# Two of a decoder layer's layer norms applied by ScalarE instead of VectorE

## The reference

```python
x = x + _L0_attn_ref(_layernorm(x), ...)      # selective scan: 512 channels, 16 states
x = x + _L0_xattn_ref(_layernorm(x), ctx_1024, ...)
x = x + _L0_ffn_ref(_layernorm(x), ...)       # RMS norm, top 2 of 8 experts

# the first part, per batch row:
xp, z = jnp.split(x @ W_in, 2, axis=-1)
xc = _silu(_causal_depthwise_conv(xp, conv_w, conv_b))
dt = softplus(xc @ W_dt + b_dt);  y = selective_scan(xc, dt, A, Bm, Cm, D)
return (y * _silu(z)) @ W_out
# the second: single-head softmax attention of the tokens over the 154 keys, + query, @ oW
```

## Time and profile before

| | us |
|---|---|
| three timed runs, median (lowest to highest) | 1635.24 (1632.82 to 1635.37) |
| the profiled execution's own time | 1633.4 |
| its span in the trace | 1631.4 |
| busy: VectorE, TensorE, GpSimd, ScalarE | 1405.1, 1249.2, 969.0, 931.2 |
| mean granted TensorE clock (share of full speed) | 0.891 |

### The profile page before, as it was taken

The page is one execution under the profiler, slowest core; times in us unless marked ns, Lnnn a source line. Parts: engine busy times, 40 slices in busy tenths (PEclk is TensorE's granted clock), DMA queues, the critical chain, the costliest instruction groups (busy, mean ns, idle before and its releaser), DMA issues. The chain is left out here.

```text
span 1631.4 us, 22872 instructions
## 1 busy us (share of the span) xinstructions
PE 1249.2 (77%) x5502; PEld 834.0 (51%) x5558; DVE 1405.1 (86%) x1861; ACT 931.2 (57%) x1369; POOL 969.0 (59%) x529
## 2 busy tenths in 40 slices
PE   4766667898677767889777687898777677797797
PEld 2344444664455445565445455566345455565465
DVE  6599999796899999787799999888699999963687
ACT  2554444146777777334777767523777767612564
POOL 1399888213888889322798889430689888620000
PEclk9877787999798989999799989999789988997699
DMA  7111110202111111201111121021111111010111
GB/s 228 41 39 43 42 45 20 99 1 80 34 58 52 46 57 53 64 26 54 59 40 58 40 71 51 27 69 54 40 41 57 58 52 60 18 61 27 45 60 52
DMA packets 54633, 86.48 MB, mean 53 GB/s; under 512 B 8572, under 2 KB 35589, under 8 KB 54542
## 3 DMA queue, kind: packets, MB, share of 16 engines
q1 hardware_dynamic: 50972, 83.20, 15.3%
q10 hardware_dynamic: 3570, 2.21, 0.5%
HBM read 74.83 MB, written 10.57 MB: 52 GB/s over the span
## 5 line engine op out<-in xcount | busy, mean ns | idle before, releaser
L1692 PE MATMUL ps<-ident,work 128*128 128x128 f32 x1536 | 309.2, 324 | 247.6 <-DVE stage L1334 170.1
L1296 DVE TENSOR_TENSOR_SCAN work<-ps,work 128x1024 f32<-128x1024 f32 x192 | 438.3, 2283 | 18.1 <-ACT ps L917 10.2
L1692 PEld LDWEIGHTS ps<-ident,work 128*128 128x128 f32 x1536 | 188.5, 159 | 383.6 <-DVE stage L1334 221.6
L917 ACT ACTIVATE ps<-dt,a_neg 128x1024 f32<-128x1024 f32 x256 | 284.8, 1117 | 121.1 <-DVE work L1296 96.3
L672 POOL TENSOR_TENSOR work<-dtu,b_bc 128x1024 f32<-128x1024 f32 x128 | 299.1, 2365 | 46.8 <-PE ps L1692 43.0
L1334 DVE SCALAR_TENSOR_TENSOR stage<-ps,c_tok,stage 128x512 f32<-128x512 f32 x384 | 272.1, 733 | 22.2 <-PE ps L1692 19.7
L1714 PE MATMUL ps<-w,work 128*128 (+1 forms) x1024 | 269.5, 411 | 1.8 <-DVE work L1441 1.8
L1714 PEld LDWEIGHTS ps<-w,work 128*128 128x128 f32 x1024 | 216.3, 213 | 52.6 <-issue 10.2
L1664 PE MATMUL ps<-nfT,w 128*128 128x512 bf16 x456 | 155.1, 430 | 40.5 <-DVE work L1371 14.6
L672 POOL TENSOR_TENSOR work<-dtu,w_out 128x1024 f32<-128x1024 f32 x64 | 149.3, 2355 | 50.1 <-PE ps L1692 50.1
L688 POOL TENSOR_TENSOR stage<-stage,work 128x512 f32<-128x512 f32 x128 | 160.5, 1277 | 11.4 <-ACT work L933 11.4
(11 more groups left out here) (164 smaller groups left out, 1879.7 us busy)
## 6 DMA issues: line engine op xcount, KB each, us to landing
b_bc<-b_rows SPq DMA_DIRECT2D x32, 512.0 KB, 3.7
w_out<-b_rows SPq DMA_DIRECT2D x32, 512.0 KB, 3.9
wbc<-combine_rows SPq DMA_DIRECT2D x64, 256.0 KB, 3.3
stage<-in_x SPq DMA_DIRECT2D x8, 512.0 KB, 4.1
xt<-in_x SPq DMA_DIRECT2D x8, 512.0 KB, 5.8
x_rows<-xt SPq DMA_DIRECT2D x4, 1024.0 KB, 4.2
res<-x_rows SPq DMA_DIRECT2D x8, 512.0 KB, 4.0
out_x<-res SPq DMA_DIRECT2D x8, 512.0 KB, 3.3
```

The costliest lines, as they stand in the source:

```text
L917: act.activation(decay_in(d, alone, opening), dt[:, d, :], ACT.Exp, scale=a_neg[:, bass.ds(it * 2 + (d * N + hf * (N // 2) + par), 1)]).th ...
L1296: dve.tensor_tensor_scan(h, decays, h, 0.0, ALU.mult, ALU.add).then_inc(scan_done, 1)
L1692: mm = pe.transpose(ps[:, a % HT_BANKS, d * P:(d + 1) * P], slot(par, d)[:, a * P:(a + 1) * P], ident[:, :])
```

## The change

`norm_apply` moves from VectorE to ScalarE for the first and the second norm: Identity(scale * x + bias) with scale = rstd and bias = -mean * rstd, both one number per token. VectorE makes the bias in place of the mean in `mv` (`norm_shift`, one SCALAR_TENSOR_TENSOR of 128x4 per half) and signals `shift_ready`. The third norm stays on VectorE. Since ScalarE now reads `mv` and `rstd`, VectorE waits for `xn_a_ready` (all 8 tiles of the first norm done) before it makes the statistics of the second where both are there. In ScalarE's program the first norm's 8 tiles stand ahead of the copies of the transposed halves; the second norm's halves stand between the evictions of `conv_in`, or, in the last stretch, each ahead of its copies and exponentials.

```diff
--- before.py
+++ after.py
@@ -244,6 +244,7 @@
 
         ve_ready = [sem(f"ve_ready{n}") for n in range(4)]
         rstd_ready = [sem(f"rstd_ready{n}") for n in range(4)]
+        shift_ready = [sem("shift_ready0"), sem("shift_ready1")]
         xn_a_ready = sem("xn_a_ready")
         xn_c_ready = sem("xn_c_ready")
         mm_ready = sem("mm_ready")
@@ -770,8 +771,15 @@
             def phases(ph):
                 r, b = ph.c_row, ph.a_row
 
-                def conv_in(d):
-                    for c in halves:
+                def norm_apply(n, src, dst, done, c):
+
+                    act.wait_ge(shift_ready[n], (b if n == 0 else r) * NH + c + 1)
+                    for a in range(c * TH, (c + 1) * TH):
+                        act.activation(dst[:, a, :], src[:, a, :], ACT.Identity, scale=rstd[:, a:a + 1],
+                                       bias=mv[:, a, 0:1]).then_inc(done, 1)
+
+                def conv_in(d, cs=halves):
+                    for c in cs:
                         ph.wait_mm(act, ("X", d, c))
                         act.activation(xp[:, d % 2, PAD + c * HALF:PAD + (c + 1) * HALF],
                                        ph.bank(("X", d, c)), ACT.Copy).then_inc(act_freed, 1)
@@ -831,11 +839,24 @@
                                            ).then_inc(gate_tanh, 1)
                 if b is not None:
                     for c in halves:
+                        norm_apply(0, xn_a, xn_a, xn_a_ready, c)
+                    for c in halves:
                         keep_normed("T", xnT, c)
                     conv_in(0)
+                if r is not None:
+                    norm_apply(1, xt, xn_c, xn_c_ready, 0)
+                    if b is not None:
+                        conv_in(1, (0,))
+                    else:
+                        keep_normed("T2", xcT, 0)
+                        score_exps(0)
+                    norm_apply(1, xt, xn_c, xn_c_ready, 1)
+                    if b is not None:
+                        conv_in(1, (1,))
+                elif b is not None:
                     conv_in(1)
                 if r is not None:
-                    for c in halves:
+                    for c in halves if b is not None else (1,):
                         keep_normed("T2", xcT, c)
                         if b is None:
                             score_exps(c)
@@ -1088,6 +1109,13 @@
                     dve.tensor_scalar(dst[:, a, :], src[:, a, :], mv[:, a, 0:1], rstd[:, a:a + 1],
                                       ALU.subtract, ALU.mult).then_inc(done, 1)
 
+            def norm_shift(ph, n, c):
+
+                row, tiles = ph.a_row if n == 0 else ph.c_row, slice(c * TH, (c + 1) * TH)
+                dve.wait_ge(rstd_ready[n], row * NH + c + 1)
+                dve.scalar_tensor_tensor(mv[:, tiles, 0], mv[:, tiles, 0], -1.0, rstd[:, tiles], ALU.mult, ALU.mult
+                                         ).then_inc(shift_ready[n], 1)
+
             def phases(ph):
                 r, b = ph.c_row, ph.a_row
 
@@ -1182,18 +1210,21 @@
                     for c in halves:
                         norm_stats(ph, 0, xn_a, c)
                     for c in halves:
-                        norm_apply(ph, 0, xn_a, xn_a, xn_a_ready, c)
+                        norm_shift(ph, 0, c)
                 if r is not None:
 
                     dve.wait_ge(xt_loaded, r * 32 + 32)
                     add_to_stream("O", 0)
+                    if b is not None:
+
+                        dve.wait_ge(xn_a_ready, b * TT + TT)
                     norm_stats(ph, 1, xt, 0)
                     add_to_stream("O", 1)
-                    norm_apply(ph, 1, xt, xn_c, xn_c_ready, 0)
+                    norm_shift(ph, 1, 0)
                     norm_stats(ph, 1, xt, 1)
                     if b is None:
                         score_max(0)
-                    norm_apply(ph, 1, xt, xn_c, xn_c_ready, 1)
+                    norm_shift(ph, 1, 1)
                 if b is not None:
                     if r is None:
```

## The result

| | before | after |
|---|---|---|
| median of 6 runs each (lowest to highest), us | 1636.07 (1632.82 to 1640.21) | 1642.09 (1640.28 to 1643.95) |
| ratio after to before, 95% interval | | 1.0035 (1.0023 to 1.0048) |
| profiled execution: own time, span | 1633.4, 1631.4 | 1640.28, 1638.5 |
| busy: VectorE, ScalarE | 1405.1, 931.2 | 1383.7, 962.0 |
| mean granted TensorE clock | 0.891 | 0.889 |

The changed kernel is 0.35% slower, 6.0 us between the medians, where 3.3 were forecast. VectorE lost 21.4 us of work and ScalarE took 30.8, and the time went up.

What follows compares the result with a forecast made beforehand. The last arrival in each stretch, not VectorE's busy share, sets the time. Opening +3.2, three middle stretches -3.0, last stretch +3.1 give +3.3 on 1635.24: 1638.5 us (own range 1637.2 to 1640.5), overall range 1633.8 to 1642.3.

Steps and rivals of the forecast that it cites:

- the statistics wait for ScalarE's eighth tile: Both-norm stretches: second norm's statistics wait about 1 us for all first-norm tiles, until 326.95, against a start at 327.10 before.
- the score maximum's waits end on TensorE: Both-norm stretches: VectorE reaches the last score maximum at about 349.9 but waits for TensorE's last score at 350.55.
- the memset comes second: Both-norm stretches: the second convolution's TENSOR_SCALAR starts at 339.1, GpSimd's memset at 339.6, a margin of half a microsecond.
- TENSOR_SCALAR is at 0.81: Both-norm stretches: the second convolution's TENSOR_SCALAR takes 0.81 us instead of 1.45, with the memset after it.
- the first rival: Both-norm stretches: GpSimd's memset precedes the second convolution, which waits until about 342.4; gain gone, about +6, 1641 us; chance 0.13.
- the tile: ScalarE: one Identity of 128x256 with scale and bias takes 0.56 us, step 0.46; bounds 0.40 and 0.58.
- ScalarE's total: Whole kernel: ScalarE's busy time rises by 64 x 0.56, 36 us.
- The gain of a middle stretch: Each of three both-norm stretches gets 1.0 us shorter, -3.0 in all; wrong if not between 0.7 and 1.3.
- The second half of T2: Both-norm stretches: TensorE's transposes of the second norm's second half run at 338.4 instead of 337.7, 0.7 late.
- The last stretch: Last stretch, second norm on the path: +3.1 us, holding the first half's +0.8; bounds +1.8 and +3.3.
- slower transposes: Last part: transposes slowed by longer idle stretches could add up to 1.5 us in any case; not in the sum.
- The opening: Opening, first norm on the path: first projection at about 19.85 instead of 16.64, +3.2 us; bounds +1.1 and +3.4.

Runs made afterwards that it cites:

- experiment 2: Changed kernel with the scale operand left out of ScalarE's Identity, so tiles are only shifted by the bias; ratio to the kernel before 0.9993.
- experiment 6: Changed kernel, last stretch reordered: second half's tiles and copies before first half's exponentials, its bias before the first maximum; 0.998. Same order with VectorE's norms: 0.9969.
- the half norm with the held memset: Kernel before with the second norm's first half on ScalarE in both-norm stretches, GpSimd's memset held until the second convolution's TENSOR_SCALAR ended; ratio 0.9947.
- the version with all three edits: Kernel before with half the second norm on ScalarE in middle stretches, memset held back, last stretch reordered with VectorE's norms; 0.9918, repeated 0.9907.

## Why the prediction was right, and where it was not

**The direction and its reason held.** Both ends lie on the path, the middle gives little back, and the sum is slower. What was forecast of the waits came true: the statistics wait for ScalarE's eighth tile and start where they did (the wait is 1.50, forecast about 1); the score maximum's waits end on TensorE; the memset comes second; TENSOR_SCALAR is at 0.81. The size was less well met: 1642.09 lies just inside the range (to 1642.3), above the forecast's own 1637.2 to 1640.5 and nearest to the 1641 of the first rival, whose mechanism didn't occur. Of the 3.6 above the forecast time, 0.8 is the kernel before, whose median over six runs is 1636.07 and not 1635.24.

**The mis-sized term is the tile.** I took 0.08 us for a pointer from rows that show 0.08 and 0.09, and a step of 0.46. It is 0.59 with a step of 0.49; experiment 2 shows 0.09 for the second. ScalarE's total rose by 30.8 and not by 36, since busy time counts the overlap of neighbours once: the two groups of tiles are busy for 16.5 and 16.2. The Trainium skill ("ScalarE: Activation LUTs", section "What ACT_TABLE_LOAD costs") gave an estimate of 0.585 and 0.49, which I had put second to my own; the trace agrees with it.

**The gain of a middle stretch: 1.0 forecast, 0.62 to 0.65 measured**, outside the 0.7 to 1.3 that I had set as a sign of being wrong. The second half of T2 was put at 338.4; it starts at 338.80. Of these 0.4 the eight tiles at 0.03 more are 0.24; 0.09 is ScalarE's later start (338.60 less 4.44 is 334.16 against 334.07); I put the rest down to semaphores, which no run shows by itself. The scores moved by the same 0.4 (350.96 against 350.55). Three stretches: 1.1 us.

**The last stretch: 3.1 forecast, 3.85 measured.** The first half's tiles are +0.9 as forecast (0.8). The transposes behind them then took 1.70 instead of 1.23, 0.5 more, after TensorE had idled 2.82 instead of 1.94; the granted clock over them was 0.60. The prediction had named slower transposes there, but left them out of the sum. The second half adds 2.4 (2.3 forecast). What costs is that the tiles stand behind exponentials: experiment 6 takes the whole loss out, and more.

**The opening: 3.2 forecast, 3.17 measured, and right by luck.** TensorE's first projection in the kernel before, which the earlier trace rows show as one row of 32, and in the kernel with only the last stretch reordered (VectorE's norms, the same opening), each row cut at about 22 us:

```profile
16.64 5.85 PE L1502 MATMUL ps<-xnT,w_in 128*128 128x512 f32 x13 [1.46 <-DMA chan<-in_D_skip]
```
```profile
16.38 6.10 PE L1503 MATMUL ps<-xnT,w_in 128*128 128x512 f32 x10 [1.42 <-DMA chan<-in_D_skip]
```

Thirteen matmuls in 5.85 us against ten in 6.10. The first convolution started at 21.19 in the one and at 22.46 in the other, and at 22.18 to 22.96 in all eight traces with this opening besides the kernel before; with ScalarE's opening it started at 24.25 to 25.17 (four traces). The means, 22.45 over nine and 24.64 over four, are 2.2 apart: that is what the move costs in the opening, and the earlier trace rows show a quick instance. From the projection's start to the convolution it took 4.55 in the kernel before and 6.08 in the other, 4.53 in the changed kernel (5.30 with ScalarE's norms at the ends alone): the forecast took this distance as fixed, and it isn't. Since the clock was granted in full in both (1.00), what slows the first matmuls is open.

**What the sum leaves.** With sizes as measured, 2.2 - 1.9 + 3.85 is +4.2 by the traces; 6.0 was timed, with an interval of 3.8 to 7.9. The 1.8 between lie within it, and no run assigns them. How far a single trace can be off from that is shown by TensorE's clock. The step sizes behind the first stretch with both norms, TensorE's timeline, before and then after; under each, the granted clock over the same sixteen matmuls (start:end, length, busy time and instructions of each engine, PEclk, DMA share, GB/s):

```profile
392.43 7.11 PE L1502 MATMUL ps<-xc,w_dt 128*128 128x512 f32 x16
...
392.40:399.40 7.00, 7.00 (x24) 3.07 (x21) 5.22 (x38) 4.50 (x7) 0.00 (x1) 1.00 0.00 0
```
```profile
396.27 10.11 PE L1533 MATMUL ps<-xc,w_dt 128*128 128x512 f32 x16
...
396.30:406.30 10.00, 10.00 (x22) 4.16 (x19) 6.17 (x39) 4.55 (x6) 1.83 (x2) 0.70 0.00 1
```

3.0 us more for the same work, at a granted clock of 0.70 against 1.00. The next stretch gave 1.8 back. A sum over three stretches read from one execution each carries this much noise, and that is why I give the stretch's own gain from entry to reciprocal, where it repeats to 0.03.

## What to carry to other kernels

An engine's total doesn't tell what a move between engines is worth: 64 tiles went from the busiest engine to a less busy one, and the time rose, since at the two ends the norm sat on the path and ScalarE is slower at it, and in the middle a third engine (TensorE) held the same point. Move only as much as the third engine's slack allows (here four tiles, not sixteen), put it ahead of what waits for others in the receiving queue, and look at what the freed engine will now meet: half the norm gained 0.0 until a memset was held back, then 1.8 per stretch. And before moving work in a chain, try its order: the last stretch gave 4.1 us by order alone, with every norm where it was. Of these 1.6 came from scores that ran at a higher granted clock once TensorE no longer waited 2.06 ahead of the transposes, so don't price such a gain by the wait alone.

## What was not expected of the hardware

- The price of a second pointer operand on ScalarE is that of the first: 128x256 in steps of 0.40 us with the bias alone, 0.49 with scale and bias.
- TENSOR_SCALAR of 128x1024 float32 beside GpSimd's memset of 128x4096 ended 0.54 us after it, wherever it began: 1.45 and 2.67 long for 0.81 of work. SCALAR_TENSOR_TENSOR beside the same memset kept its 3.92 for three. It works the other way round too: with the bias alone, TENSOR_SCALAR began 0.24 ahead of the memset and kept its 0.81, and the memset took 4.03 instead of 3.51. The Trainium skill ("SBUF — State Buffer", section "Who interferes with whom") has the blocking as a rule; the traces agree.
- TensorE's granted clock can be lower where TensorE has waited less. In the half norm with the held memset the scores ended where they did, its offset of 1.69 taken off, and the transposes of the probabilities began 1.8 earlier, after an idle time of 2.04 us instead of 3.78; the first projections behind them took 1.92 instead of 1.03, and 1.7 of the gain was lost there. TensorE in the kernel before, then in that kernel, with the window over these projections:

```profile
357.02 1.03 PE L1598 MATMUL ps<-w_qo,dt 128*128 128x256 f32 x4
...
356.00:362.00 6.00, 6.00 (x31) 5.38 (x31) 5.86 (x6) 2.44 (x4) 0.00 (x0) 0.94 0.01 3
```
```profile
357.16 1.92 PE L1628 MATMUL ps<-w_qo,dt 128*128 128x256 f32 x4
...
356.00:362.00 6.00, 6.00 (x20) 5.11 (x19) 5.86 (x5) 2.25 (x3) 0.00 (x0) 0.56 0.00 0
```

The clock was granted at 0.56 there and at 0.94 before. It came in the first stretch of that trace and not in the second or third (from the reciprocal to the step sizes the offset grew by 1.7, -0.2, 0.0); in both traces of the version with all three edits it came in the first and the third, 1.8 each. So it repeats, but isn't a rule of this order; what decides it stays open.
